# Second biases of the four experts in one weighted product a step, and the first block prepared while self-attention runs out

## What is computed

```python
x = x + cross_attention(layernorm(x), ctx)      # x: 128 x 32 x 128, ctx: 128 x 257 x 128
x = x + self_attention(layernorm(x))            # 16 heads, 32 tokens
x = x + ffn(layernorm(x))

def moe_layer(x, rw, rb, g, b, w1, b1, w2, b2):  # ffn: 4 such layers, each with 4 experts
    probs = softmax(x @ rw + rb)                 # 128 -> 4
    vals, idx = top_k(probs, 2); vals = vals / vals.sum()
    xhat = layernorm(x)
    xe = xhat * g[e] + b[e]
    h = gelu(xe @ w1[e] + b1[e])                 # 128 -> 512, for all four experts
    y = h @ w2[e] + b2[e]                        # 512 -> 128
    comb = vals at idx, zero elsewhere
    return sum_e comb[e] * (x + y[e])
```

## Time and profile before

| | |
|---|---|
| median of 3 runs (lowest, highest) | 1393.75 us (1386.02, 1393.91) |
| the profiled execution | 1394.39 us, span 1391.7 us |
| busy share of the span | PE 93%, DVE 84%, ACT 80%, POOL 51% |
| chain that ended last, by engine | PE 46%, DVE 3%, issue 2%, ACT 1% |
| mean granted TensorE clock | 0.967 of full speed |

### The profile page before, as it was taken

How to read it: one execution, slowest core, us unless ns; L and a number is a source line. 1 busy time by engine, 2 the same in 40 slices (tenths; PEclk the granted TensorE clock), 3 DMA queues, 4 the chain that set the end, 5 groups by cost and what they waited for, 6 DMA issues and landing times.

```text
span 1391.7 us, 45724 instructions
## 1 busy us (share of the span) xinstructions
PE 1292.1 (93%) x15671; PEld 976.8 (70%) x15671; DVE 1167.6 (84%) x3416; ACT 1114.4 (80%) x1886; POOL 712.9 (51%) x557
## 2 busy tenths in 40 slices
PE   5898999999997699986999999999999999999998
PEld 3676778778776588843767667777777777777776
DVE  4799988999998689887999988788878887889885
ACT  3598999999996657655898978888888888888886
POOL 7276777777776865531444433333333333333333
PEclk9899999999998679997999999999999999999999
DMA  5875766766763288800000000000000000000000
GB/s 157 231 211 161 188 187 181 191 185 186 195 172 90 42 216 219 220 14 1 2 1 0 0 1 1 0 0 0 0 0 0 0 0 0 2 8 15 8 17 16
DMA packets 196207, 108.54 MB, mean 78 GB/s; under 512 B 89740, under 2 KB 194028, under 8 KB 196076
## 3 DMA queue, kind: packets, MB, share of 16 engines
q1 hardware_dynamic: 122032, 84.65, 21.9%
q10 hardware_dynamic: 74044, 22.17, 7.2%
HBM read 67.62 MB, written 39.03 MB: 77 GB/s over the span
## 4 chain that ended last, share of the span: by engine, by line
PE 46%; DVE 3%; issue 2%; ACT 1%; DVEq 0%; ACTq 0%
PE pair L1787 22%; PE pair L1769 20%; PE pair L1776 2%; PE pair L1808 1%; PE pair L1799 1%; DVE hs L1693 1%; ACT gf L1614 0%; DVE w1p L1046 0%; DVE gl L1679 0%; DVE w2p L1050 0%; DVE rw L38 0%; DVE st L1640 0%; DVE xl L1740 0%; ACT gh L1619 0%; DVE rs L53 0%
## 5 line engine op out<-in xcount | busy, mean ns | idle before, releaser
L1601 POOL TENSOR_TENSOR gl<-gf,gh 128x1024 f16<-128x1024 f32 x128 | 286.5, 2239 | 480.4 <-ACT gh L1619 480.4
L1614 ACT ACTIVATE gf<-pair,b1c 128x512 f32<-128x512 f32 x512 | 327.2, 680 | 98.3 <-PE pair L1769 97.0
L1787 PE MATMUL pair<-w2p,gh 128*128 (+1 forms) x4096 | 357.3, 219 | 0.0
L1787 PE MATMUL pair<-w2p,gl 128*128 (+1 forms) x2048 | 349.6, 219 | 0.0
L1769 PE MATMUL pair<-xh,w1p 128*128 128x512 f16 x1024 | 329.2, 383 | 9.8 <-ACT gf L1614 8.2
L1787 PEld LDWEIGHTS pair<-w2p,gh 128*128 128x128 f16 x4096 | 319.7, 98 | 23.0 <-issue 0.4
L405 POOL TENSOR_TENSOR pl<-p,ph 128x1024 f16<-128x1024 f32 x128 | 273.1, 2134 | 118.5 <-ACT ph L462 118.4
L1619 ACT ACTIVATE gh<-gf 128x1024 f16<-128x1024 f32 x256 | 270.6, 1057 | 24.0
L1679 DVE SCALAR_TENSOR_TENSOR gl<-gf,gh 128x1024 f16<-128x1024 f32 x128 | 160.8, 1256 | 83.5 <-ACT gh L1619 81.3
L1787 PEld LDWEIGHTS pair<-w2p,gl 128*128 128x128 f16 x2048 | 200.3, 98 | 0.0
L1769 PE MATMUL pair<-xl,w1p 128*128 128x512 f16 x512 | 196.1, 383 | 0.0
(11 more groups left out here) (240 smaller groups left out, 2448.8 us busy)
## 6 DMA issues: line engine op xcount, KB each, us to landing
KS<-k_parts_dram SPq DMA_DIRECT2D x64, 384.0 KB, 4.4
k_parts_dram<-kh SPq DMA_DIRECT2D x64, 256.0 KB, 3.4
cx<-in_ctx_dram ACTq DMA_DIRECT2D x30, 512.0 KB, 4.5
k_parts_dram<-kl SPq DMA_DIRECT2D x64, 128.0 KB, 3.6
w1p<-in_L_ffn_w_dram SPq DMA_DIRECT2D x8, 512.0 KB, 5.8
w2p<-in_L_ffn_w_dram SPq DMA_DIRECT2D x8, 512.0 KB, 7.6
QS<-q_parts_dram ACTq DMA_DIRECT2D x128, 24.0 KB
K<-k_parts_dram SPq DMA_DIRECT2D x8, 384.0 KB
```

The costliest lines, as they stand in the source:

```text
L1601: pool.tensor_tensor(gl[u.m2][:, 0:h, :], gf[u.m2][:, 0:h, :], gh[u.m2][:, 0:h, :], ALU.subtract).then_inc(d_loP, 1)
L1614: act.activation(gf[u.m2][:, c, :], hb[c][:, :], ACT.Gelu, scale=1.0 / WS, bias=b1c[:, u.step.expert(u.e), c]).then_inc(d_g, 1)
L1787: last = pe.matmul(yb[v.m2][:, t * D:(t + 1) * D], g[:, c, t * P:(t + 1) * P], w2p[:, le, part, c, :].rearrange("p a h -> p (a h)"), start ...
```

## The change

Second biases. The product L1776 in every unit is taken out. Instead, once a step, the four weights of each token are written in float16 parts into `c16` (two more small VectorE instructions in the new `weigh`), TensorE transposes `c16` (unit 1), ScalarE copies the result (`cT16`, start of unit 2), TensorE multiplies it with `b2R`, a block-diagonal matrix of the layer's four biases for four tiles (one product of 512 columns, unit 3, into `tbk`), and VectorE adds the product to `hs` in one instruction over four tiles (`add_bias`, after the third `combine`). `b2R` is built in the drain: four products of TensorE in turn (6, 0) and four copies of ScalarE.

First block. The gelu's bias columns now come straight from products of one column (64 of them, four to an expert, with float32 first weights as the stationary side) in turns (6, 2) to (7, 3), so that copy, transposes and their wait are gone. In the drain VectorE also computes the deviations of blocks 0 and 1 in one pass and `xc` of block 0, TensorE transposes it, and ScalarE loads the gelu's table by a one-column instruction. The normalised input `hs` is made by ScalarE throughout, spread from turn (7, 3) to step 2; the late part of its statistics (`attended_late`) moves from the lead-in to step 1. The weights of experts 2 and 3 are split by VectorE in step 0 instead of the drain; step 0's `comb` is made after its first gelus, so that they no longer stand behind the routing. Steps 1 to 6 are written out instead of looped. (Below, the indentation of each piece of the diff is cut.)

```diff
-pick = sb(whole, "pick", [P, LE, P], F16)
+b2R = sb(whole, "b2R", [P, L, 4 * D], F16)
...
-if at == (NBLK, 1):
-    act.wait_ge(c_s, HEAD + 4)
-    act.wait_ge(e_ln, HEAD + RSTD_STEPS + 1)
-    for t in range(FIRST_HS):
-        attended(act, t)
-if at in ((NBLK, 1), (NBLK, 2)):
-    high_weights(act, 1 + w)
-if at == (NBLK, 3):
-    act.wait_ge(e_b1, LE)
-    act.activation(b1r[:, :], bank[1][0:LE, 0:F], ACT.Copy).then_inc(e_cols, 1)
...
+        if at in ((6, 1), (6, 2)):
+            act.wait_ge(e_T, 3)
+            act.wait_ge(e_pick, 5)
+            for t in (2 * w - 2, 2 * w - 1):
+                own = slice(32 * t, 32 * t + 32)
+                act.activation(b2R[own, :, t * D:(t + 1) * D], bank[0][own, :].rearrange("p (l d) -> p l d", l=L), ACT.Copy)
+        if at == (7, 3):
+            act.wait_ge(c_s, HEAD + 4)
+            act.wait_ge(e_ln, HEAD + RSTD_STEPS + 1)
+        if at in ATTENDED:
+            for t in range(*ATTENDED[at]):
+                attended(act, t)
+        if at == (NBLK, 0):
+            act.activation(warm[:, :], gain[:, 0:1], ACT.Gelu)
+        if at in ((NBLK, 0), (NBLK, 1)):
+            high_weights(act, 2 + w)
+ATTENDED = {(7, 3): (0, 4), (NBLK, 0): (4, 8), (NBLK, 1): (8, 12)}
...
+if at in ((7, 3), (NBLK, 0)):
+    le = (w + 1) % 4
+    dve.wait_ge(e_b1, LE)
+    low_weights(dve, le)
...
+            dve.wait_ge(d_hs, 8)
+            for k in range(8):
+                dve.bn_stats(st8[:, k, :], hs[:, k, :]).then_inc(d_ln, 1)
+            dve.wait_ge(d_ln, 8)
+            dve.tensor_tensor(b1c[:, :, :].rearrange("p x c -> p (x c)"), bank[1][:, 0:LE * FC],
+                              cols[:, 64:64 + LE * FC], ALU.add)
+            for k in range(8):
+                dve.bn_aggr(mv8[:, k // 4, k % 4, :], st8[:, k, :]).then_inc(d_ln, 1)
+        if at == (NBLK, 2):
+            flat = lambda r: r[:, :, :].rearrange("p i k -> p (i k)")
+            dve.wait_ge(d_ln, 16)
+            inverse_deviation(dve, seed, flat(rs8), flat(rw8), flat(rt8),
+                              mv8[:, :, :, 1].rearrange("p i k -> p (i k)"), d_ln, 16)
+            for k in range(4):
+                dve.tensor_scalar(xc[:, k, :], hs[:, k, :], mv8[:, 0, k, 0:1], rs8[:, 0, k:k + 1],
+                                  ALU.subtract, ALU.mult).then_inc(d_x, 1)
 blocks(step, prepare)(dve)
-dve.wait_ge(e_T, 2)
-dve.tensor_tensor(b1c[:, :, :].rearrange("p x c -> p c x"),
-                  bank[0][:, 0:FC * LE].rearrange("p (c x) -> p c x", c=FC),
-                  cols[:, 64:64 + LE * FC].rearrange("p (x c) -> p c x", c=FC), ALU.add)
...
+        if at == (6, 0):
+            pe.wait_ge(c_vn, NBLK)
+            pe.wait_ge(e_pick, 5)
+            pe.wait_ge(e_b2, 3)
+            for l in range(L):
+                last = pe.matmul(bank[0][:, l * D:(l + 1) * D], place[:, l, :, :, :].rearrange("p t g e -> p (t g e)"),
+                                 b2p[:, :], start=True, stop=True)
+            last.then_inc(e_T, 1)
         if at in BIAS1:
             pe.wait_ge(e_w, WLOAD)
-            pe.wait_ge(e_cols, 3)
+            pe.wait_ge(e_cols, 2)
             pe.wait_ge(c_lo, 2 * NBLK)
             for le in range(*BIAS1[at]):
-                pe.matmul(bank[1][0:LE, 0:F], lnbd[:, le, :], w1f[:, le + SHIFT, :], start=(le == 0),
-                          stop=(le == LE - 1)).then_inc(e_b1, 1)
-BIAS1 = {(6, 2): (0, 1), (6, 3): (1, 2), (7, 0): (2, 3), (7, 1): (3, 4), (7, 2): (4, 6), (7, 3): (6, 8),
-         (8, 0): (8, 10), (8, 1): (10, 12), (8, 2): (12, 14), (8, 3): (14, 16)}
+                for c in range(FC):
+                    last = pe.matmul(bank[1][:, le * FC + c:le * FC + c + 1], w1f[:, le + SHIFT, c * P:(c + 1) * P],
+                                     cols[:, 32 + le:33 + le], start=True, stop=True)
+                last.then_inc(e_b1, 1)
+BIAS1 = {(6, 2): (0, 2), (6, 3): (2, 4), (7, 0): (4, 7), (7, 1): (7, 10), (7, 2): (10, 13), (7, 3): (13, LE)}
 blocks(step)(pe)
-pe.wait_ge(e_cols, 4)
-pe.wait_ge(c_vn, NBLK)
-for c in range(FC):
-    last = pe.transpose(bank[0][:, c * LE:(c + 1) * LE], b1r[:, c * P:(c + 1) * P], ident[0:LE, 0:LE])
-last.then_inc(e_T, 1)
+pe.wait_ge(d_x, 4)
+pe.wait_ge(c_oc, NT)
+for k in range(4):
+    last = pe.transpose(bank[6][:, k * P:(k + 1) * P], xc[:, k, :], ident[:, :])
+last.then_inc(d_xT, 1)
...
-    if f and e == 3:
-        act.wait_ge(d_r, RSTEPS * (f.n + 1))
+    if f and e == 1 and not u:
+        for t in range(12, 16):
+            attended(act, t)
+    at = (u.step.n, e) if u and isinstance(u.step.n, int) else None
+    if at in LATER:
+        if LATER[at][0] == HEAD:
+            act.wait_ge(e_ln, HEAD + RSTD_STEPS + 1 + NT - HEAD + RSTD_STEPS + 1)
+        for t in range(*LATER[at]):
+            attended(act, t)
+    weighed = u.step if at == (0, 0) else f if u and f and e == 3 else None
+    if weighed:
+        act.wait_ge(d_r, RSTEPS * (weighed.n + 1))
         act.activation(th[:, :, :], z[:, :, :], ACT.Tanh).then_inc(d_th, 1)
-for t in range(FIRST_HS, HEAD):
-    attended(act, t)
+LATER = {(1, 1): (16, 20), (1, 3): (20, 24), (2, 1): (24, 28), (2, 3): (28, NT)}
 steps(act, unit, high_weights)
...
-dve.wait_ge(d_acc, 4 * v.n + ACC0)
+wait(dve, d_acc, ADDS * v.step.n + 4 * v.e + (v.e == E - 1))
...
+def weigh(f):
+    dve.tensor_scalar(sel2[:, :, :], sel[:, :, :], 0.5 / WS, None, ALU.mult).then_inc(d_c16, 1)
+    dve.wait_ge(d_c16, 3 * f.n + 2)
+    dve.wait_ge(d_th, f.n + 1)
+    dve.scalar_tensor_tensor(comb[f.m2][:, :, :], th[:, :, :], 1.0, sel2[:, :, :],
+                             ALU.add, ALU.mult).then_inc(d_comb, 1)
+    dve.wait_ge(d_comb, f.n + 1)
+    wait(dve, d_tc, f.n)
+    dve.tensor_scalar(c16[:, :, 0:3:2, :], comb[f.m2][:, :, :].unsqueeze(2).broadcast_to((P, 4, 2, E)), WS, None,
+                      ALU.mult).then_inc(d_c16, 1)
+    dve.wait_ge(d_c16, 3 * f.n + 3)
+    dve.scalar_tensor_tensor(c16[:, :, 1, :], comb[f.m2][:, :, :], WS, c16[:, :, 0, :],
+                             ALU.mult, ALU.subtract).then_inc(d_c16, 1)
+def add_bias(s):
+    t = hs[:, bass.ds(4 * s.block, 4), :].rearrange("p t c -> p (t c)")
+    dve.wait_ge(d_P, s.n + 1)
+    dve.wait_ge(d_acc, ADDS * s.n + 4 * (E - 1))
+    dve.scalar_tensor_tensor(t, tbk[:, :], 1.0 / WS, t, ALU.mult, ALU.add).then_inc(d_acc, 1)
 def unit(u, v, f, third, e, final):
-    if f and e == 0:
-        if not u:
-            deviations(f)
+    at = (u.step.n, e) if u and isinstance(u.step.n, int) else None
+    opening = at is not None and at[0] == 0
+    if u and f and e == 0:
         normalise(f, final)
-    if third and e == 1 and u:
+    if u and third and e == 1 and not opening:
         deviations(third)
     if f and e == 1:
         dve.wait_ge(d_xh, f.n + 1)
         dve.tensor_tensor(xl[f.m2][:, :], tbk[:, :], xh[f.m2][:, :], ALU.subtract).then_inc(d_xl, 1)
-    if third and e == 1 and not u:
-        deviations(third)
-        attended_late()
     if u:
         low_half(u)
+    if at == (0, 0):
+        low_weights(dve, 2)
+        weigh(u.step)
+    if opening and e == 2:
+        deviations(third)
     if f and e == 2:
         route(f)
     if v:
         combine(v, final)
-    if f and e == 3:
-        dve.tensor_scalar(sel2[:, :, :], sel[:, :, :], 0.5 / WS, None, ALU.mult).then_inc(d_comb2, 1)
-        dve.wait_ge(d_comb2, f.n + 1)
-        dve.wait_ge(d_th, f.n + 1)
-        dve.scalar_tensor_tensor(comb[f.m2][:, :, :], th[:, :, :], 1.0, sel2[:, :, :],
-                                 ALU.add, ALU.mult).then_inc(d_comb, 1)
+    if u and e == 3:
+        add_bias(u.step)
+    if at == (0, 1):
+        low_weights(dve, 3)
+    if at == (1, 2):
+        attended_late()
+    if u and f and e == 3:
+        weigh(f)
+dve.memset(c16[:, :, :, :].rearrange("p t g e -> p (t g e)"), 0.0).then_inc(d_c16, 1)
+dve.wait_ge(d_c16, 1)
 steps(dve, unit, low_weights, lead=True)
...
-wait(pe, d_acc, 4 * v.n + (ACC0 - 4))
+wait(pe, d_acc, ADDS * v.step.n + (4 * (v.e - 1) if v.e >= 2 else 4 * (v.e + 3) + (v.e == 1) - ADDS))
 le = v.step.expert(v.e)
-pe.matmul(yb[v.m2][:, :], pick[:, le, :].rearrange("p a m -> p (a m)"),
-          b2p[:, :].unsqueeze(1).broadcast_to((P, 4, D)), start=True, stop=False,
-          skip_group_check=True)
+if isinstance(v.n, int) and v.n in (2, 3):
+    pe.wait_ge(e_lo2, v.n + 1)
...
+if u and f and e == 1:
     pe.wait_ge(d_x, 4 * f.n + 4)
     wait(pe, d_xl, f.n)
+    wait(pe, d_acc, ADDS * (f.n - 2) + ADDS - 4)
...
     last.then_inc(d_lg, 1)
+if u and e == 3:
+    if f:
+        pe.wait_ge(d_xl, f.n + 1)
+    pe.wait_ge(d_cc, u.step.n + 1)
+    pe.matmul(tbk[:, :], cT16[:, :], b2R[:, bass.ds(u.step.layer, 1), :].rearrange("p a m -> p (a m)"),
+              start=True, stop=True).then_inc(d_P, 1)
 if v:
     outputs(v)
+if u and e == 1:
+    pe.wait_ge(d_c16, 3 * u.step.n + 4)
+    pe.transpose(lbk[:, 64:128].bitcast(F16), c16[:, :, :, :].rearrange("p t g e -> p (t g e)"),
+                 ident16[:, :]).then_inc(d_tc, 1)
```

150 lines of the change are left out of this document (78 added, 72 removed).

## The result

After the change the median is 1427.51 us (1419.29 to 1429.78), before it 1393.35, measured side by side: 1.0247 times as long, 95% interval 1.0193 to 1.0301. The forecast was 1375.5 (1363 to 1388). The profiled execution took 1428.86 with a span of 1427.1, 35.4 more than the span before. TensorE is 91% busy instead of 93, its mean granted clock 0.946 instead of 0.967.

A forecast was written before the change was run, and what follows sets the result against it. TensorE was taken to bound the kernel. Drain -12.6, steps 0 to 2 +5, steps 3 to 6 0 and steady steps -10.8 made -18.4 from 1394.39: 1376.0, as median 1375.5 us, range 1363 to 1388.

The forecast's parts named there:

- Bias columns: Drain: 64 one-column float32 products, 128 TensorE instructions, taking 9.3 us in all; turn (7, 3) ends 2.1 later.
- The cheap end: Drain: lower price of a one-column instruction, from L1407's 16 columns: 0.0725 us at full clock, 9.3 in all; the forecast used it.
- rival A: Drain: one column costs as much as 128 through weight loads, up to 0.133 us an instruction; +4.7, total 1380.1; chance 0.14.
- the dear end: Drain: upper price of a one-column instruction, from L1460's 128 columns: 0.133 us, 17.0 in all; turn (7, 3) ends 9.8 later.
- The chain behind it: End of drain: `hs` tiles, statistics and `xc` lead to the experts' first product at 631.0 instead of 632.17; drain term -12.6.
- Steps 0 to 2: Moved splits, late statistics and bias work give VectorE 8.8 us more, partly into 4.5 idle: +5, ends 3 and 9.
- Steps 3 to 6: Each gets 1.0 us of VectorE work into 1.5 idle and loses the loop's register work: 0, ends -3 and +3 together.
- Steady steps: Steps 7 to 31: three products leaving and one coming count, 0.43 us less a step, -10.8 in 25 steps.
- Price 0: Steady steps: `xc`, held by GpSimd, ends at 1025.2, before TensorE transposes it at 1026.3; 1.1 us of cover, no cost.
- Last layer: No term of its own: counted with the steady steps at 0.43 us less each; -3.0 for steps 23 to 29.
- Rival D: Every step: VectorE, held by GpSimd, becomes the bound; 24.2 us a step, +26 over 25 steps, about 1413; chance 0.06.

The follow-up runs named there:

- cols64: Changed kernel with 64 moving columns instead of one in each of the gelu's 64 bias products, the other results unread; 1409.52 us, 1.0120 times the kernel before.
- cols_as_before: Changed kernel with the gelu's bias columns made as before (16-row products, copy, four transposes); 1411.45 us, 1.0109 times the kernel before.
- no_bias2: Changed kernel without any second bias in the steps (no `c16`, transpose, copy, product or `add_bias`); 1400.73 us, 1.0041 times the kernel before.
- one_split: cols_as_before with one expert's split a step in steps 2 to 13, behind unit 2, instead of two in 1 to 6; steps 1 to 14 written out; 1385.66 us, 0.9942.
- one_split_pick_all: one_split with second biases by the product in every unit throughout, as before the change; 1378.45 us, 0.9888 times the kernel before.
- one_split_pick_last: one_split with second biases by the product in every unit from step 23 on, without `c16` and `add_bias` there; 1380.06 us, 0.9897 times the kernel before.
- dev_sum_later: dev_later with the last layer's addition of `xs` also moved, to the end of unit 0; 1430.56 us, 1.0253 times the kernel before.
- dev_later: cols_as_before with VectorE's inverse root moved behind `xl` and `low_half`; 1434.47 us, 1.0288 times the kernel before.

## Why the prediction was wrong, by its steps

- **Bias columns.** The step that failed: "I take the cheap end, since one column is nearer to 16 than to 128". Columns were the wrong scale: at full clock an instruction takes the same with one column (0.108) as with 64 (0.110), and the weight loads are busy all the time (8.00 of 8.00 us in cols64), as rival A has it. The cheap end itself was a misreading: the 0.29 of L1407's pair holds only one load, and its second instruction took 0.22 at half clock. And both ends were worked out for full clock, while these products ran mostly at half: 0.207, above the dear end. The row at 16 columns had a clock of 0.50 as well; I halved it instead of asking why. Size: step 0 comes 6.2 later instead of 12.6 earlier, a miss of 18.8, of which cols_as_before gives back 18.6.
- **The chain behind it** (eight `hs`, statistics, `xc`, first product) was right: 630.37 measured in cols_as_before, 631.0 forecast.
- **Steps 0 to 2.** Right in kind, +12.0 instead of +5 and over the far end of 9: I filled VectorE's idle time with work, but the waits come one behind another (`c16`, `hs`, `xl`, `gl`), 10.6 in all, and 3.1 more go to the lower clock.
- **Steps 3 to 6.** The step that failed: "get 1.0 each of work into 1.5 of idle time ... 0, ends -3 and +3". Measured +12.6. Idle time is not what decides there: VectorE has the splits and GpSimd's `gl` to get past, and where holds fell on instructions ahead of `xl`, TensorE stood 4.79 (step 4) and 4.36 (no_bias2).
- **Steady steps.** 0.43 was right where no hold stands on the way (one_split against one_split_pick_all), to the hundredth by luck, since the transpose left out and the router's wait put too high cancel; in the kernel's loops 0.30 came of it, since L38 is still held and the router waits 0.43. "Price 0" for `xc`'s lateness held there.
- **Last layer.** I counted its steps with the steady ones. They carry the addition of `xs` on VectorE besides, and with `add_bias` and `c16` `low_half` falls behind `gl`: +10.1 instead of -3.0. Without `add_bias` and `c16` there these steps are 11 shorter (one_split_pick_last against one_split); moving the addition alone gave 1.9 (dev_sum_later against dev_later).
- **Rival D** named the mechanism that made the kernel slower, VectorE held by GpSimd until it bounds the step, but set it in every step and at 0.06. It came in steps 0 to 6 and 23 to 29, which have something more on VectorE, and left the others alone. The rows for it stood in the forecast: VectorE 22.19 of 23.70 in a split step, and a wait of 0.85 there already.

Open stays what in the loop shifts the holds, why the split steps alternate between a shorter and a longer form, and how much of the cure is the number of splits in a step and how much their place.

## What to carry to other kernels

A very narrow product is not cheap for its columns: it costs a weight load, and a drain full of them ran at half TensorE's clock, with all that stood among them, so look at the granted clock of the row that you scale from, and leave out the first instruction of a run, whose load may lie behind the product ahead. Where two engines hold one another, do not add work to "idle time" before asking which instruction will start just behind the other engine's long one and who waits for it; the stages with most work on the held engine decide, not the steady one. Here, where such a stage was over full, spreading its work over more steps gained and reordering it lost.

## What the runs showed of the hardware that was not expected

- TensorE busy 10.00 of 10 us, with its weight load busy 10.00 too, at a granted clock of 0.50; 64 columns in place of one, or 448 more in between, gave 1.00.
- A VectorE instruction of 0.16 us with its operands in SBUF takes up to 2.11 if it starts 0.03 behind GpSimd's `gl`; a `combine` (PSUM operand) and statistics beside a `gl` keep 1.12 and 0.86. Where VectorE is first, GpSimd's `gl` is the one that grows, from 2.14 to as much as 3.31 in the kernel after. The Trainium skill ("SBUF — State Buffer", section "Who interferes with whom") says it in a sentence: "Issue order, not op shape, decides who blocks." The rows above agree.
- The same working instructions took 22.26 a step written out and 22.92 to 23.24 in a loop (one_split), where TensorE waited for `xl` (0.20) and `xc` (0.35) in the window shown.
